# Norm attention layers: q and k turned by VectorE blocks and a DRAM trip, the score mask added on VectorE

## Chip, cores and metric

The kernel is one launch on one core of a Trainium2 chip. The metric is device time in microseconds, median over runs. TensorE is called PE below, VectorE DVE, ScalarE ACT, GpSimd POOL, and SyncE, which here issues most DMAs, SP.

## What is computed

Eight sublayers on `x` (8 batch elements b, 128 tokens, 512 columns): four times cross attention and a feed-forward part, each `x = x + tanh(g) * f(layernorm(x))`. The attention of layers 0, 1 and 3 has 32 query heads in 8 groups that share k and v, heads of 128. Layer 0 rotates q and k by position, layers 1 and 3 normalise them (layer 2 has small heads, and its code is another):

```python
q = rmsnorm((hidden_states @ q_proj_w.T).reshape(B, Q, NUM_HEADS, HEAD_DIM).transpose(0, 2, 1, 3), q_norm_w)
k = rmsnorm(jnp.repeat(k, n_rep, axis=1), k_norm_w)       # k, v from cross_attention_states
scores = jnp.einsum('bhqd,bhkd->bhqk', q, k) * scale + attention_mask
attn = jax.nn.softmax(scores.astype(jnp.float32), axis=-1).astype(q.dtype)
out = jnp.einsum('bhqk,bhkd->bhqd', attn, v)
return out.transpose(0, 2, 1, 3).reshape(B, Q, NUM_HEADS * HEAD_DIM) @ o_proj_w.T
```

The feed-forward parts are a LoRA mixture (0), a quantised matmul (1), and mixtures of experts with dispatch (2, 3).

## The kernel before

**Split operands.** Every fp32 operand of a matmul is kept as a high and a low part in fp32r: ACT copies the high part, DVE or POOL subtracts it from the source for the low part, and a product is three matmuls (high-high, high-low, low-high).

**Units.** In layers 0, 1 and 3 the work is cut into 64 units, unit u being group u // 8 and batch element u % 8: project q (4 heads), k and v into a PSUM bank pair (L806 by `keys_values` and `project`), normalise or rotate q and k into `qk` (L1592), transpose the five 128x128 pieces on PE (`turn_q`, four L852 into `B_qT` and one L855), split q and k into high and low (ACT L1162, DVE L1474 and L1615), scores (L863, L864), mask, maximum, exponentials (L1333), division by the sum (POOL L2222), turn P, P times v (L883), split of the result o, projection to the output (L806 into `B_out`) and addition to `X` (L1650).

**The mask.** ACT copies the low half of the scores, scaled, from PSUM to `S` (`low_scores`); POOL adds the mask (L2183); DVE adds the high half (`mask`, L1622) and takes the maximum (L1625).

**Turning P.** All but 8 units turn P without PE: DVE transposes blocks of 32x32 (`blocks_p`, L1640), SP stores them to DRAM (`store_p`, L2367) and loads them back in another order (`load_p`, L2372), ACT and POOL split the result (`split_p`, L2228).

**The order.** The class `Schedule` writes one order for all engines. Unit u has its home step i = first + u; `at(i, order, name, ...)` puts an operation into step i at a place between 0 and 100. One list comes out, sorted by step and place, and each engine takes from it the operations that it has a part in and runs them in that order, waiting on semaphores. So in a steady step i PE runs attn_out of unit u-6, times_v of u-5, scores of u-2, turn_q of u-1, and the projections of u. Operation `next` splits a landed half of a weight (256 KB; 10 halves each 8 units) and asks SP for the next; in steady steps one at place 15 gives the low part to DVE, one at 90 to POOL.

**Between stages** (the first and last 8 units of a layer), layer norms and feed-forward parts are put among the units.

## Time and profile before

| | us |
|---|---|
| median of 3 runs | 2618.07 (2617.1 to 2621.32) |
| span of the profiled execution | 2614.6 |
| PE busy | 2382.5 (91%) |
| DVE busy | 1786.3 (68%) |
| POOL busy | 1512.2 (58%) |
| ACT busy | 1278.9 (49%) |

Busy times are of the one profiled execution. Engines run side by side, so the times don't add up to the span, and a share over the whole span mixes stages with different limits. An engine that is busy all of a stretch is its bound there.

### The profile page before, as it was taken

The page shows a single profiled execution, that of the slowest core. Times are in us where ns is not written, and L with a number is a line of the kernel's source. Part 1 is how long each engine was busy: PE and PEld are TensorE (multiplying, and loading weights), DVE is VectorE, ACT ScalarE, POOL GpSimd, SP SyncE. Part 2 cuts the span into 40 slices and gives each one's busy share as a digit, 9 for nine tenths or more (in the row PEclk, how much of TensorE's full clock was granted, in tenths as well). Part 3 has the DMA queues.
Part 4 walks back from the last instruction along what each step waited for, and adds up shares of the span by engine and source line. Part 5 has one row for each costly group of instructions (what it writes and reads, how often), then busy time and mean ns, then how long its engine had stood idle before and what let it go on. Part 6 is the DMA issues. An engine that isn't in the chain of part 4 may idle for free.

```text
span 2614.6 us, 41410 instructions
## 1 busy us (share of the span) xinstructions
PE 2382.5 (91%) x13005; PEld 2016.6 (77%) x13005; DVE 1786.3 (68%) x3406; ACT 1278.9 (49%) x3698; POOL 1512.2 (58%) x1567
## 2 busy tenths in 40 slices
PE   5899999998889999999887887899689999999977
PEld 4788888886778888888766776776578888888753
DVE  4677777777877777777666676563477777777752
ACT  2555555554246666666534455233245666665421
POOL 5666666665246666666535667423456666666543
PEclk9999999999999999999999999899889999999979
DMA  3234444443224233223310000259513233322344
GB/s 110 80 118 155 141 160 159 151 162 109 71 84 142 97 98 102 93 93 98 109 49 17 1 1 27 81 193 365 175 61 108 91 98 101 101 94 77 116 169 151
DMA packets 191532, 288.12 MB, mean 110 GB/s; under 512 B 15985, under 2 KB 110833, under 8 KB 188378
## 3 DMA queue, kind: packets, MB, share of 16 engines
q1 hardware_dynamic: 175584, 236.34, 27.1%
q0 software_dynamic: 10224, 42.03, 4.6%
q10 hardware_dynamic: 5514, 7.11, 0.9%
q8 instruction: 112, 1.84, 0.3%
q14 instruction: 98, 0.80, 0.1%
HBM read 218.80 MB, written 100.37 MB: 122 GB/s over the span
## 4 chain that ended last, share of the span: by engine, by line
PE 73%; DVE 8%; DMA 6%; POOL 5%; issue 4%; ACT 3%; SPq 0%; POOLq 0%; ACTq 0%; DVEq 0%
PE B_qkv L806 32%; PE B_out L806 19%; PE B_more L883 4%; PE B_s L863 4%; PE B_qT L852 3%; DMA slots_y<-S 3%; PE B_more L806 2%; PE B_s L864 1%; PE B_more L957 1%; DMA out_x<-rows_last 1%; PE B_s L806 1%; DVE xn L1523 1%; DVE X L1650 1%; PE B_qT L806 1%; PE B_more L855 1%
## 5 line engine op out<-in xcount | busy, mean ns | idle before, releaser
L1333 ACT ACTIVATE W<-S,nmx 128x128 f32<-128x128 f32 x768 | 298.1, 395 | 49.9 <-DVE nmx L1625 48.8
L2183 POOL TENSOR_TENSOR S<-S,mask 128x512 f32<-128x512 f32 x184 | 256.6, 1394 | 46.9 <-ACT S L1162 46.9
L1226 ACT ACTIVATE sq<-B_qkv 128x640 f32<-128x640 f32 x127 | 89.7, 706 | 380.1 <-PE B_qkv L806 380.1
L2228 POOL TENSOR_TENSOR pT_l<-W,pT_h 128x512 fp32r<-128x512 f32 x184 | 241.8, 1314 | 32.9 <-ACT pT_h L1162 30.7
L2157 POOL TENSOR_SCALAR rn<-ss 128x5 f32<-128x5 f32 x128 | 25.3, 198 | 371.3 <-DVE ss L1563 371.3
L806 PE MATMUL B_qkv<-ring_h,xnT_h 128*128 128x512 f32 x540 | 216.2, 400 | 11.3 <-DVE spare_l L1474 4.8
L2222 POOL TENSOR_TENSOR W<-W,rden 128x512 f32<-128x512 f32 x192 | 202.1, 1052 | 32.7 <-DVE rden L1630 32.6
L806 PE MATMUL B_qkv<-ring_l,xnT_h 128*128 128x512 f32 x540 | 214.5, 397 | 0.0
L806 PE MATMUL B_out<-ring_h,oT_h 128*128 128x512 f32 x516 | 206.1, 399 | 8.7 <-DVE kT L1615 4.4
L806 PE MATMUL B_qkv<-ring_h,xnT_l 128*128 128x512 f32 x540 | 212.8, 394 | 0.0
L863 PE MATMUL B_s<-kT,qT_h 128*128 128x256 f32 x768 | 191.1, 326 | 17.8 <-DVE xnT_l L1474 15.1
L806 PE MATMUL B_out<-ring_l,oT_h 128*128 128x512 f32 x516 | 205.7, 399 | 0.0
L806 PE MATMUL B_out<-ring_h,oT_l 128*128 128x512 f32 x516 | 202.6, 393 | 0.0
L1563 DVE TENSOR_REDUCE ss<-sq 128x5 f32<-128x640 f32 x128 | 105.1, 821 | 140.8 <-ACT sq L1226 140.7
L1650 DVE SCALAR_TENSOR_TENSOR X<-B_out,gates,X 128x512 f32<-128x512 f32 x200 | 149.0, 745 | 42.3 <-PE B_out L806 42.3
L2149 POOL TENSOR_TENSOR ring_l<-raw,ring_h 128x512 fp32r<-128x512 f32 x107 | 144.2, 1351 | 50.4 <-ACT ring_h L1162 50.3
L864 PE MATMUL B_s<-kT,qT_l 128*128 128x128 f32 x768 | 172.0, 224 | 0.0
L1640 DVE STREAM_TRANSPOSE S<-W 128x512 f32<-128x512 f32 x184 | 129.4, 703 | 62.1 <-POOL W L2222 62.1
L863 PEld LDWEIGHTS B_s<-kT,qT_h 128*128 128x128 f32 x768 | 146.1, 190 | 29.5 <-issue 21.8
L1162 ACT ACTIVATE oT_h<-B_more 128x512 fp32r<-128x512 f32 x200 | 119.6, 598 | 97.6 <-PE B_more L883 94.6
L806 PE MATMUL B_qkv<-ring_h,ctxT_h 128*128 128x256 f32 x540 | 165.0, 306 | 0.0
L2160 POOL TENSOR_TENSOR rn<-rn,pw 128x5 f32<-128x5 f32 x128 | 151.1, 1181 | 10.7
(514 smaller groups left out, 7730.5 us busy)
## 6 DMA issues: line engine op xcount, KB each, us to landing
raw<-in_pieces SPq DMA_DIRECT2D x270, 256.0 KB, 2.6
between_p<-S SPq DMA_DIRECT2D x184, 256.0 KB, 2.2
W<-between_p SPq DMA_DIRECT2D x184, 256.0 KB, 2.8
slots_x<-in_zero SPq DMA_DIRECT2D x32, 1030.0 KB, 6.0
raw<-in_experts SPq DMA_DIRECT2D x16, 768.0 KB, 6.5
w<-in_experts SPq DMA_DIRECT2D x8, 1024.0 KB, 14.0
slots_y<-S SPq DMA_DIRECT2D x31, 256.0 KB, 6.4
xn<-slots_x ACTq DMA_DIRECT2D x8, 257.5 KB, 5.8
```

What stands on the lines that cost most here:

```text
L806: t = pe.matmul(dst, a, b, start=first and n == 0, stop=last and n == len(steps) - 1)
L863: pe.matmul(B_s[:, cols(r, 2 * P)], qT[0][:, cols(r)], kT_both[:, :], start=True, stop=False)
L864: t = pe.matmul(B_s[:, cols(2 * r)], qT[1][:, cols(r)], kT[0], start=False, stop=True)
L1162: return act.activation(dst, src, ACT.Copy, scale=scale)
L1333: t = act.activation(W[:, k, cols(r)], S[:, k, cols(r)], ACT.Exp, bias=nmx[:, k, r:r + 1], accum_out=den[:, k, r:r + 1])
L1640: dve.transpose(blocks_first(S[:, k, :]), W[:, k, :].rearrange("p (r j q) -> p r j q", r=R, q=BLOCK)).then_inc(*blocks_made.now((layer, u)))
L1650: dve.scalar_tensor_tensor(out=X[:, b, 0:D], in0=bank[:, :], scalar=factor, in1=X[:, b, 0:D], op0=ALU.mult, op1=ALU.add).then_inc(*x_add.n ...
L2149: pool.tensor_tensor(lo, landing_place(item), f32(hi), ALU.subtract).then_inc(*piece_lo["pool"].now(i))
L2160: pool.tensor_tensor(rn[:, k, 0:R + 1], rn[:, k, 0:R + 1], pw[:, 0:R + 1], ALU.pow).then_inc(*rms.now((layer, u)))
L2183: pool.tensor_tensor(S3, S3, m.unsqueeze(1).to_broadcast([P, R, P]), ALU.add).then_inc(*masked.now((layer, u)))
L2222: pool.tensor_tensor(W3, W3, rden[:, k, :].unsqueeze(2).to_broadcast([P, R, P]), ALU.mult).then_inc(*probs.now((layer, u)))
L2228: pool.tensor_tensor(heads_first(pT[1][:, :]), by_block(W[:, k, :]), heads_first(f32(pT[0][:, :])), ALU.subtract).then_inc(*p_split.now((l ...
```

## The change

For units 8 to 59 of layers 1 and 3 (`TURNED_BY_DMA`) q and k are no longer turned by PE. DVE transposes 32x32 blocks of `qk` into `xn` (`blocks_q`), SP stores them to DRAM and loads them back (`store_q`, `load_q`, 320 KB each, the load in runs of 640 bytes) into a new tile `q_in`. ACT scales k by the norm weights in place and copies the high parts, DVE makes k's low part, POOL q's (`split_q`). Their projections alternate between two bank pairs, `B_qkv` and the banks that `B_qT` and P's turning had. The order of these units is new: scores come behind the projection of two units later (place 70.5), mask and maximum at 4 of the next step, exponentials at 16, the block transpose and store of P at 42 of the same step. In these steps the weight split at place 15 goes to POOL.

For all units of layers 0, 1 and 3 ACT's copy of the low scores and POOL's addition of the mask are gone: DVE makes two passes from PSUM instead of one (scaled low half plus mask, then the high half), and the maximum stands in an operation of its own directly behind them.

Smaller parts: the 8 units whose P is turned by PE write their exponentials in turned order; the norm weights come in two orders of rows; the routers' weights are loaded later, and share their place with `q_in`; waits for the last q store and split stand ahead of what reuses `xn` and that place.

```diff
@@ -56,6 +56,8 @@
 AHEAD = tuple((0, u) for u in range(1, 5))
+TURNED_BY_DMA = {(layer, u) for layer in (1, 3) for u in range(NB, G * NB - 4)}
+LAST_BY_DMA = G * NB - 5
...
@@ -152,24 +154,42 @@
                 self.at(i + 1, 6 if layer == 1 and u < NB else 10, "normalise", layer, u)
-            self.at(i + 1, 50, "turn_q", layer, u)
-            self.at(i + 1, 50, "split_k", layer, u)
-            self.at(i + 2, 40, "scores", layer, u)
-            self.at(i + 2, 41, "low_scores", layer, u)
-            self.at(i + 2, 56, "mask", layer, u)
-            self.at(i + 2, 71, "exp", layer, u)
-            self.at(i + 3, 9, "probs", layer, u)
-            if (layer, u) in TURNED_BY_PE:
-                self.at(i + lag - 2, 46 if u == 0 and (layer, 1) in AHEAD else 30, "turn_p", layer, u)
+            if (layer, u) in TURNED_BY_DMA:
+                self.at(i + 1, 10.2, "blocks_q", layer, u)
+                self.at(i + 1, 12, "store_q", layer, u)
+                self.at(i + 1, 41, "load_q", layer, u)
+                self.turns_by_dma.add(i + 2)
+                self.at(i + 2, 13, "split_k", layer, u)
+                self.at(i + 2, 13.5, "split_q", layer, u)
+                self.at(i + 2, 70.5, "scores", layer, u)
+                self.at(i + 3, 4, "mask", layer, u)
+                self.at(i + 3, 4, "max", layer, u)
+                self.at(i + 3, 16, "exp", layer, u)
+                self.at(i + 3, 40, "probs", layer, u)
+                self.at(i + 3, 42, "blocks_p", layer, u)
+                self.at(i + 3, 42, "store_p", layer, u)
+                self.at(i + 3, 73, "load_p", layer, u)
+                self.at(i + 4, 45, "split_p", layer, u)
             else:
-                self.at(i + 3, 21, "blocks_p", layer, u)
-                self.at(i + 3, 21, "store_p", layer, u)
-                self.at(i + 3, 62, "load_p", layer, u)
-                self.at(i + lag - 2, 60, "split_p", layer, u)
+                self.at(i + 1, 72 if (layer, u - 1) in TURNED_BY_DMA else 50, "turn_q", layer, u)
+                self.at(i + 1, 72 if (layer, u - 1) in TURNED_BY_DMA else 50, "split_k", layer, u)
+                self.at(i + 2, 40, "scores", layer, u)
+                self.at(i + 2, 56, "mask", layer, u)
+                self.at(i + 2, 56, "max", layer, u)
+                self.at(i + 2, 71, "exp", layer, u)
+                self.at(i + 3, 9, "probs", layer, u)
+                if (layer, u) in TURNED_BY_PE:
+                    self.at(i + lag - 2, 46 if u == 0 and (layer, 1) in AHEAD else 30, "turn_p", layer, u)
+                else:
+                    self.at(i + 3, 21, "blocks_p", layer, u)
+                    self.at(i + 3, 21, "store_p", layer, u)
+                    self.at(i + 3, 62, "load_p", layer, u)
+                    self.at(i + lag - 2, 60, "split_p", layer, u)
             self.at(i + lag - 1, 20, "times_v", layer, u)
             self.at(i + lag, 0, "attn_out", layer, u, needs=five[3:5],
                     frees=[(n, "attn_out", (layer, u), i + lag) for n in five[3:5]] if last else ())
-            self.at(i + lag, 10.5 if KINDS[layer] == "norm" else 0, "add_out", layer, u)
+            self.at(i + lag, 10.5 if KINDS[layer] == "norm" else 0,
+                    "add_out", layer, u)
...
@@ -413,13 +433,23 @@
             for order in ((71, 90) if i < 7 else (15, 90) if i in self.steady else (5, 24, 46, 90)):
-                self.at(i, order, "next", i + order / 100, "dve" if order in (15, 46) else "pool")
+                if i in self.turns_by_dma and order == 15:
+                    self.at(i, order, "split_piece", i + order / 100)
+                    self.at(i, 42.5, "fetch_piece", i + order / 100)
+                else:
+                    self.at(i, order, "next", i + order / 100, "dve" if order == 46 else "pool")
         for i in range(end + 1):
             for _, _, name, args, needs, frees in sorted(self.events[i], key=lambda x: x[:2]):
                 if name == "next":
                     now, engine = args
...
@@ -593,18 +625,21 @@
         between_p = [nc.dram_tensor(f"between_p{k}", (P * HG,), F32).ap() for k in range(2)]
+        between_q = [nc.dram_tensor(f"between_q{k}", (P * (HG + P),), F32).ap() for k in range(2)]
         scales = [tables[:, :, :].rearrange("p a n -> p (a n)")[:, h * HALF:(h + 1) * HALF] for h in range(2)]
         B_qkv = pb("B_qkv", 1024)
-        B_qT = pb("B_qT", 512)[:, :]
         B_s = pb("B_s", 1024)
         B_sc, B_kT = B_s[:, 0:512], B_s[:, 512:1024]
-        B_more = pb("B_more", 1024)
-        B_pt, B_oT = B_more[:, 0:512], B_more[:, 512:1024]
+        B_three = pb("B_three", 1536)
+        B_qT, B_pt, B_oT = (B_three[:, k * 512:(k + 1) * 512] for k in range(3))
+        B_more, B_other = B_three[:, 512:1536], B_three[:, 0:1024]
         def unit_bank(layer, u):
-            return (B_more, ("pt", "oT")) if (layer, u) in ASIDE else (B_qkv, ("qkv",))
+            if (layer, u) in ASIDE:
+                return B_more, ("pt", "oT")
+            return (B_other, ("qT", "pt")) if u % 2 and (layer, u) in TURNED_BY_DMA else (B_qkv, ("qkv",))
...
@@ -1240,15 +1291,28 @@
                 kind = KINDS[layer]
-                act.wait_ge(*qk_turned.of((layer, u)))
+                by_dma = (layer, u) in TURNED_BY_DMA
+                act.wait_ge(*(q_loaded[unit(layer, u)[3]] if by_dma else qk_turned).of((layer, u)))
                 for sem, value in qT_reader:
                     act.wait_ge(sem, value)
                 if layer == 3 and u == 0:
                     act.wait_ge(*kbd_made2.of(NB - 1))
-                scale = wqk[:, layer // 2:layer // 2 + 1] if kind == "norm" else 1.0
+                scale = key_weights(layer, u) if kind == "norm" else 1.0
                 if kind == "norm" and u == 0:
                     act.wait_ge(*const.of("wqk"))
-                copy(key_rows(layer, u, kT[0]), key_columns(layer, u), scale).then_inc(*kT_hi.now((layer, u)))
+                if by_dma:
+                    if kind == "norm":
+                        copy(keys_in, keys_in, scale).then_inc(*k_scaled.now((layer, u)))
+                        act.wait_ge(*k_scaled.of((layer, u)))
+                    copy(keys_by_part(kT[0]), keys_in).then_inc(*kT_hi.now((layer, u)))
+                else:
+                    copy(block_keys(kT[0]), turned_keys(key_bank(layer, u)[0]), scale).then_inc(*kT_hi.now((layer, u)))
+            def split_q(layer, u):
+                act.wait_ge(*q_loaded[unit(layer, u)[3]].of((layer, u)))
+                for sem, value in qT_reader:
+                    act.wait_ge(sem, value)
+                copy(heads_first(qT[0][:, :]), queries_in).then_inc(*qT_hi.now((layer, u)))
...
@@ -1311,26 +1377,16 @@
-            def low_scores(layer, u):
-                k = unit(layer, u)[3]
-                act.wait_ge(*scored.of((layer, u)))
-                if layer == 0 and u == 0:
-                    act.wait_ge(*const.of("mask0"))
-                if layer == 3 and u < 2:
-                    for t in range(TILES2 - 2, TILES2):
-                        act.wait_ge(*y_stored[t % 2].of((2, t)))
-                elif k in S_reader:
-                    act.wait_ge(*S_reader[k])
-                copy(per_head(S[:, k, :]), score_parts[:, :, 1, :], SCALE).then_inc(*low_scored.now((layer, u)))
             def exp(layer, u):
                 kind, g, b, k, vs = unit(layer, u)
                 act.wait_ge(*maxed.of((layer, u)))
                 for token in W_reader.get(k, ()):
                     act.wait_ge(*token)
...
@@ -1604,23 +1665,54 @@
+            def blocks_q(layer, u):
+                k = unit(layer, u)[3]
+                dve.wait_ge(*{"rope": roped, "norm": normed}[KINDS[layer]].of((layer, u)))
+                if u == NB:
+                    dve.wait_ge(*ln_turned.of((f"attn{layer}", NB - 1)))
+                else:
+                    dve.wait_ge(*q_stored[1 - k].of((layer, u - 1)))
+                dve.transpose(blocks_first(q_turns), qk[:, :].rearrange("p (h j q) -> p h j q", j=BLOCKS, q=BLOCK)
+                              ).then_inc(*q_blocks.now((layer, u)))
             def split_k(layer, u):
+                kind = KINDS[layer]
+                if (layer, u) in TURNED_BY_DMA:
+                    turned, (hi, lo) = keys_in, (keys_by_part(m) for m in kT)
+                else:
+                    turned, (hi, lo) = turned_keys(key_bank(layer, u)[0]), (block_keys(m) for m in kT)
+                dve.wait_ge(*kT_hi.of((layer, u)))
+                if kind == "rope" or (layer, u) in TURNED_BY_DMA:
+                    sub(lo, turned, f32(hi)).then_inc(*kT_lo.now((layer, u)))
+                else:
+                    dve.scalar_tensor_tensor(out=lo, in0=turned, scalar=key_weights(layer, u), in1=f32(hi),
+                                             op0=ALU.mult, op1=ALU.subtract).then_inc(*kT_lo.now((layer, u)))
+            def mask(layer, u):
                 kind, g, b, k, vs = unit(layer, u)
-                bank = key_columns(layer, u)
-                hi, lo = (key_rows(layer, u, m) for m in kT)
-                dve.wait_ge(*kT_hi.of((layer, u)))
-                if kind == "rope":
-                    sub(lo, bank, f32(hi)).then_inc(*kT_lo.now((layer, u)))
-                else:
-                    dve.scalar_tensor_tensor(out=lo, in0=bank, scalar=wqk[:, layer // 2:layer // 2 + 1], in1=f32(hi),
-                                             op0=ALU.mult, op1=ALU.subtract).then_inc(*kT_lo.now((layer, u)))
-            def mask(layer, u):
+                S3 = per_head(S[:, k, :])
+                m = mask0[:, b, :] if kind == "rope" else mask13[:, :]
+                dve.wait_ge(*scored.of((layer, u)))
+                if layer == 0 and u == 0:
+                    dve.wait_ge(*const.of("mask0"))
+                if layer == 1 and u == 0:
+                    dve.wait_ge(*small["mask13"].of(0))
+                if layer == 3 and u < 2:
+                    for t in range(TILES2 - 2, TILES2):
+                        dve.wait_ge(*y_stored[t % 2].of((2, t)))
+                elif k in S_reader:
+                    dve.wait_ge(*S_reader[k])
+                S_reader[k] = (exped if (layer, u) in TURNED_BY_PE else p_stored[k]).of((layer, u))
+                dve.scalar_tensor_tensor(out=S3, in0=score_parts[:, :, 1, :], scalar=SCALE, in1=m.unsqueeze(1).to_broadcast([P, R, P]),
+                                         op0=ALU.mult, op1=ALU.add).then_inc(*low_masked.now((layer, u)))
+                dve.wait_ge(*low_masked.of((layer, u)))
+                dve.scalar_tensor_tensor(out=S3, in0=score_parts[:, :, 0, :], scalar=SCALE, in1=S3, op0=ALU.mult, op1=ALU.add
+                                         ).then_inc(*sc_read.now((layer, u)))
+            def largest(layer, u):
                 k = unit(layer, u)[3]
                 S3 = per_head(S[:, k, :])
-                dve.wait_ge(*masked.of((layer, u)))
-                dve.scalar_tensor_tensor(out=S3, in0=score_parts[:, :, 0, :], scalar=SCALE, in1=S3, op0=ALU.mult, op1=ALU.add
-                                         ).then_inc(*sc_read.now((layer, u)))
...
@@ -2168,19 +2261,10 @@
-            def low_scores(layer, u):
-                    pool.tensor_tensor(S3, S3, m.unsqueeze(1).to_broadcast([P, R, P]), ALU.add).then_inc(*masked.now((layer, u)))
+            def split_q(layer, u):
+                pool.wait_ge(*qT_hi.of((layer, u)))
+                pool.tensor_tensor(heads_first(qT[1][:, :]), queries_in, heads_first(f32(qT[0][:, :])), ALU.subtract
+                                   ).then_inc(*q_low.now((layer, u)))
...
@@ -2372,6 +2456,27 @@
+            def store_q(layer, u):
+                k = unit(layer, u)[3]
+                sync.wait_ge(*q_blocks.of((layer, u)))
+                if q_loaded[k].made:
+                    sync.wait_ge(q_loaded[k].sem, q_loaded[k].by * q_loaded[k].made)
+                sync.dma_start(between_q[k].rearrange("(p n) -> p n", p=P), q_turns).then_inc(*q_stored[k].now((layer, u)))
+            def load_q(layer, u):
+                k = unit(layer, u)[3]
+                sync.wait_ge(*q_stored[k].of((layer, u)))
+                if u > NB:
+                    sync.wait_ge(*q_low.of((layer, u - 1)))
+                    sync.wait_ge(*kT_lo.of((layer, u - 1)))
+                elif layer == 1:
+                    sync.wait_ge(*ffn0_done.of(NB - 1))
+                elif layer == 3:
+                    sync.wait_ge(*v_group2.of((NB - 1, G - 1)))
+                    sync.wait_ge(*logits.of(("ffn2", NB - 1)))
+                sync.dma_start(q_in[:, :, :], between_q[k].rearrange("(i p n) -> p i n", i=BLOCKS, p=P)
+                               ).then_inc(*q_loaded[k].now((layer, u)))
...
```

## Rows read from the trace of the kernel before

**Rows 1.** The page's first line.

```profile
span 2614.6 us, 41410 instructions
```

**Rows 2.** Busy us (x instructions) by stretch: PE, PEld, DVE, ACT, POOL; clock; DMA share; GB/s.

```profile
300.00:400.00 100.00, 100.00 (x576) 87.73 (x575) 71.89 (x140) 54.98 (x170) 67.29 (x63) 1.00 0.43 144
900.00:1000.00 100.00, 100.00 (x576) 87.69 (x575) 72.67 (x127) 60.52 (x177) 64.08 (x62) 1.00 0.28 88
2150.00:2250.00 100.00, 100.00 (x576) 87.69 (x575) 73.97 (x128) 61.55 (x179) 65.65 (x62) 1.00 0.29 95
```

**Rows 3.** The same view, between layers 0 and 1.

```profile
590.00:770.00 180.00, 149.12 (x801) 125.94 (x800) 141.44 (x334) 63.85 (x188) 71.46 (x86) 0.94 0.26 88
```

**Rows 4.** Timeline of PE (start us, us, engine, line, operation) around one unit's transposes.

```profile
1014.44 0.61 PE L852 MATMUL B_qT<-ident,qk 128*128 128x128 f32 x4
...
1015.12 0.28 PE L806 MATMUL B_qkv<-ring_lent_l,ctxT_h 128*128 128x256 f32 x1
1015.24 0.28 PE L806 MATMUL B_qkv<-ring_lent_h,ctxT_l 128*128 128x256 f32 x1
```

**Rows 5.** Timeline of ACT, the exponentials of two units in a row.

```profile
1002.03 0.40 ACT L1333 ACTIVATE W<-S,nmx 128x128 f32<-128x128 f32 x1
...
1011.09 0.40 ACT L1333 ACTIVATE W<-S,nmx 128x128 f32<-128x128 f32 x1
...
1012.62 0.62 ACT L1162 ACTIVATE ring_h<-raw 128x512 fp32r<-128x512 f32 x1
```

**Rows 6.** Timeline of DVE over one unit; in brackets the idle time before and its releaser.

```profile
1009.16 0.67 DVE L1622 SCALAR_TENSOR_TENSOR S<-B_s,S 128x512 f32<-128x512 f32 x1
1009.87 0.69 DVE L1625 TENSOR_REDUCE nmx<-S 128x4 f32<-128x512 f32 x1
1011.07 0.82 DVE L1563 TENSOR_REDUCE ss<-sq 128x5 f32<-128x640 f32 x1 [0.51 <-ACT sq L1226]
1011.80 0.28 DVE L1474 TENSOR_TENSOR v_l<-B_qkv,v_h 128x128 fp32r<-128x128 f32 x1
1012.76 0.18 DVE L1630 RECIPROCAL rden<-den 128x4 f32<-128x4 f32 x1 [0.68 <-ACT W L1333]
1013.47 0.82 DVE L1592 TENSOR_TENSOR qk<-B_qkv,rn 128x640 f32<-128x640 f32 x1 [0.53 <-POOL rn L2160]
1014.21 0.74 DVE L1650 SCALAR_TENSOR_TENSOR X<-B_out,gates,X 128x512 f32<-128x512 f32 x1
1014.87 0.68 DVE L1474 TENSOR_TENSOR ring_l<-raw,ring_h 128x512 fp32r<-128x512 f32 x1
1015.47 0.68 DVE L1474 TENSOR_TENSOR oT_l<-B_more,oT_h 128x512 fp32r<-128x512 f32 x1
1016.07 0.70 DVE L1640 STREAM_TRANSPOSE S<-W 128x512 f32<-128x512 f32 x1
...
1017.27 0.33 DVE L1615 SCALAR_TENSOR_TENSOR kT<-B_more,wqk,kT 128x128 fp32r<-128x128 f32 x1
```

**Rows 7.** Timeline of DVE and POOL, a weight split beside a POOL instruction.

```profile
1005.60 1.04 POOL L2222 TENSOR_TENSOR W<-W,rden 128x512 f32<-128x512 f32 x1
...
1005.82 1.37 DVE L1474 TENSOR_TENSOR ring_l<-raw,ring_h 128x512 fp32r<-128x512 f32 x1
```

**Rows 8.** Groups of 800 to 1200 us: busy us, mean ns, idle before.

```profile
L2183 POOL TENSOR_TENSOR S<-S,mask 128x512 f32<-128x512 f32 x44 | 67.6, 1537 | 13.9 <-ACT S L1162 13.9
...
L2228 POOL TENSOR_TENSOR pT_l<-W,pT_h 128x512 fp32r<-128x512 f32 x45 | 58.3, 1295 | 1.1 <-ACT pT_h L1162 0.7
...
L1162 ACT ACTIVATE pT_h<-W 128x512 fp32r<-128x512 f32 x44 | 27.8, 633 | 0.9 <-DMA W<-between_p 0.9
```

**Rows 9.** SP's timeline of one trip of P, and time to landing of the loads.

```profile
1008.44 0.33 SPq L2367 DMA_DIRECT2D between_p<-S  x1
1010.49 0.38 SPq L2372 DMA_DIRECT2D W<-between_p  x1
...
DMA to landing us min/median/max: 2.5/2.7/5.8
```

93 lines of the change are left out of this document (57 added, 36 removed).

## Prediction

> **What bounds the kernel now.** I read the page's first section, then busy time by stretch, then the timelines of one unit (one batch element of one group of heads), engine by engine, then the waits and DMA landings. The span is 2614.6 us [rows 1]; the median of the runs is 2618.07, so 3.5 us more. By stretch [rows 2] TensorE (PE) is busy 100.00 of 100.00 us in the middle of layers 1 and 3, at a granted clock of 1.00 (the 2.4 GHz level), while VectorE (DVE) has 73 to 74, ScalarE (ACT) about 61 and GpSimd (POOL) about 65. So there only less work on PE saves time, until another engine or a loop of waits needs longer than PE. Between stages [rows 3] it is the other way round: in 590 to 770 PE loses 31 us and DVE is busy 141 of 180.
> One unit takes 9.06 us: ACT's exponentials start at 1002.03 and, one unit on, at 1011.09 [rows 5].
>
> **PE, the gain.** A unit now has five transposes, four L852 and one L855. The first starts at 1014.44; the second matmul of the projection behind them starts at 1015.12 [rows 4]; L855 and the first matmul lie between. Matmuls of 256 columns follow each other by 0.12 (1015.12 to 1015.24), so the five take 1015.12 - 0.12 - 1014.44 = 0.56 us. They go in units 8 to 59 of layers 1 and 3: 2 x 52 = 104 units, 104 x 0.56 = **58 us**. All of it lies where PE is the bound. A unit of PE alone would then take 9.06 - 0.56 = **8.50 us**. Moving scores behind the next projection adds no PE work; the alternating second bank lets the projection start without the normalisation before it.
>
> **DVE's loop, the first thing that may come late.** DVE works in order, and the block transpose of P (blocks_p) now stands in the same step as the exponentials it follows. From one reduction of squares to the next, in the new order, start to start from [rows 6]: reduction 0.73, v low 0.21, two mask passes 0.71 each (0.67 and a gap of 0.04 since each waits for the one before), maximum 0.62, normalisation 0.86 (0.82 and the gap; otherwise a start comes 0.07 before the end of the one ahead), new blocks_q 0.81 (640 columns where the shown transpose has 512 and 0.70: 0.88, less 0.07 overlap), add to X 0.66, k low 0.25, o low 0.60, reciprocal 0.18, then POOL's 1.04 [rows 7] with 0.12 for its two semaphores (an estimate from the 0.04 gap on DVE, taken larger since it crosses engines), blocks_p 0.62. Sum **8.12 us**. The second mask pass is bounded by its like, the pass of L1622 at 0.67, and by the 0.74 of L1650, also PSUM with SBUF. The exponentials (1011.09 to the next ACT instruction at 1012.62: 1.53 [rows 5]) start when the maximum is out, and o's copy follows them, about 2.1 in all; DVE has 0.86 + 0.81 + 0.66 + 0.25 = 2.58 to do meanwhile, so "o behind the exponentials" is covered with 0.4 to spare. Were this cover gone, each late 0.1 us would count.
> Also gone from DVE: q's low part and its share of weight splits (now all POOL's in these units).
> An unknown: k's low part now reads two SBUF operands. DVE's weight split with two SBUF operands took 0.68 alone and 1.37 when a POOL instruction was under way [rows 6, 7]. POOL gets the weight splits and q's low part (by its like, L2228, 1.30) and loses the mask addition of 1.54 [rows 8]: -1.54 + 1.30 + about 0.6 splits of 1.30 = +0.54 a unit, on about 65 / 100 x 9.06 = 5.9, so 6.4 busy of 8.5. Bounds of the wait: 0 and a whole POOL instruction of 1.30. I take 0.4 on average, since a POOL split stands at that place in about 6 of 10 units: 8.12 + 0.4 = 8.52, about PE's 8.50. **Taken: 8.52 a unit, 104 x (9.06 - 8.52) = 56 us saved.**
> The Trainium skill (SBUF — State Buffer, "SBUF: two separate sides") says that a DVE instruction with two SBUF inputs and a GpSimd instruction that reads SBUF exclude each other, the later one waiting for the whole of the other. The trace agrees: 0.68 against 1.37. By the rule k's low part, 0.33 with a PSUM source, could take up to 1.6.
>
> **The trip's loop, the second.** ACT's split_k and split_q now stand before the exponentials, so ACT waits for the loaded q with the exponentials behind it; on them hang DVE's reciprocal, blocks_p, the next reduction and two steps later blocks_q. That closes a loop over two units: reduction to the end of blocks_q 4.72; store 2.05 for P (issue 1008.44, the waiting load at 1010.49 [rows 9]), taken 2.2 for a quarter more bytes; load 2.7 [rows 9], taken 2.9; ACT's k scaling, k copy and q copy 1.3 (an estimate: P's copy of the same 512 columns takes 0.63, k's with 128 about half [rows 8]); exponentials 1.53, o's copy 0.67, then o low, reciprocal, POOL, blocks_p 2.56. Sum 15.9 in two units, **8.0 a unit**: hidden by 0.5 a unit. Bounds for the load: 2.5 and 5.8, the shortest and longest of P's. SP is queued too: store_q, load_q, store_p, the weight load, load_p; behind store_q's wait stand the weight loads, but each of its two trips blocks it about 2.2 us, and it then has 4 us for its other issues of 0.33 to 0.38. Scores (PE) want q's low part about 7.7 into the loop; POOL has it at about 5.
>
> **The mask, all 192 units.** ACT's copy and POOL's addition go, DVE gets 0.67. Inside the full stretches it is in the 8.12; in layer 0 DVE goes from 71.89 / 100 x 9.06 = 6.5 to 7.2 a unit, hidden. In the ramps between stages it isn't surely hidden: about 38 units lie there, 38 x 0.67 = 25 us if all of it counts; below nothing, -5, if the shorter way to the maximum matters more (DVE waited there only a few us for POOL's mask addition). I take 7, about ten units at the 79% busy DVE of 590 to 770. The exponentials' turned writes in 8 units, the wider constants, the late load of the routers: nothing, in shade of PE.
> **Entering and leaving** the new order, four times: bounds 0 and 3 us each (one late DMA trip); I take 3 in all.
>
> **Sum.** -56 + 7 + 3 = -46: the profiled span 2614.6 becomes 2569, the median 2618.07 becomes **2572**.
>
> **Rivals.**
> *Port.* k's low part meets POOL in every unit and waits half an instruction, 0.65: 8.77 a unit, 104 x 0.29 = 30 saved, -30 + 10: **2598**. For it: POOL is busy three quarters of the time. Against: outside the splits POOL is idle just then. The rule cited above makes this one; it needs only the rows.
> *The trip comes late (slower).* If store and load need 7.3 us together instead of 5.1, the two-unit loop is 18.1 and the gain gone; from there it costs. With loads at P's longest, 5.8, it is 18.9: 9.43 a unit, 104 x 0.37 = +38, with the ramps +10: **2666**. For it: a weight load may be on the wire with each, and SP's order lets a late weight split hold back store_q. Against: P's own trips show a median of 2.7 with the same weight loads about, and the DMA share is 0.29 [rows 2].
> *The ramps eat it.* The full 25 us there and 4 x 3 for entering: -56 + 37: **2599**.
> *Nothing in the way.* 58 saved, ramps -2: **2558**.
>
> **Chances.** Forecast (2560 to 2590) 0.52, port 0.14, ramps 0.10, nothing in the way 0.06, late trip 0.12, and 0.06 that several small losses add up to no change. A measurement here can tell 0.2%, 5 us, from no change. Late trips split 0.10 slower and 0.02 same; the small losses 0.05 same and 0.01 slower; 0.01 same and 0.03 slower come out of the port and ramp cases at their upper ends. So faster 0.78, same 0.08, slower 0.14. The range reaches from below the free case to just over no change: 2555 to 2622; the likeliest one's own is 2560 to 2590.
>
> **What would show it.** PE matmuls in a full 100 us stretch: 52 a unit become 47; at 8.5 us a unit 553 instead of 576 matmuls, PE still near 100. If PE is under 98 there, a loop binds: then look at what PE waits for. Waits of ACT's k copy for the DMA into q_in mean the late trip; k's low part over 0.5 us on DVE means the port; reductions directly behind blocks_p with no idle time mean DVE's loop. Between stages, DVE's share and PE's lost time tell the ramps. I would be wrong most of all if the unit stays over 8.8.

## The result, and the profile after

The changed kernel takes 2585.5 us (median of 4 runs, 2585.0 to 2594.8) beside 2619.4 us of the kernel before on the same chip: ratio 0.9885, 95% interval 0.9867 to 0.9903, which is 25 to 35 us of 2619 (the medians lie 34 apart). The forecast was 2572, 46 us faster. The profiled execution's span went from 2614.6 [rows 1] to 2584.0, 30.6 us; the account below is made against that.

From the page of the changed kernel: first line, busy time by engine, the chain that ended last by engine, and the DMA issues (count, KB each, us to landing):

```profile
span 2584.0 us, 40807 instructions
PE 2344.7 (91%) x12485; PEld 1968.5 (76%) x12485; DVE 1860.3 (72%) x3505; ACT 1231.8 (48%) x3610; POOL 1480.0 (57%) x1572
...
PE 21%; POOL 13%; DMA 12%; DVE 10%; issue 9%; ACT 4%; SPq 0%; POOLq 0%; DVEq 0%; ACTq 0%
...
between_p<-S SPq DMA_DIRECT2D x184, 256.0 KB, 2.5
W<-between_p SPq DMA_DIRECT2D x184, 256.0 KB, 2.8
between_q<-xn SPq DMA_DIRECT2D x104, 320.0 KB, 2.6
q_in<-between_q SPq DMA_DIRECT2D x104, 320.0 KB, 3.0
```

The chain is no longer one engine's: PE's share was 73% before. Busy time by stretch, the columns of rows 2 and the stretches of rows 2 and 3:

```profile
300.00:400.00 100.00, 100.00 (x576) 87.68 (x575) 75.87 (x144) 48.71 (x157) 59.40 (x58) 1.00 0.45 143
900.00:1000.00 100.00, 100.00 (x549) 86.26 (x548) 84.98 (x141) 64.74 (x189) 74.11 (x73) 1.00 0.54 172
2150.00:2250.00 100.00, 98.76 (x537) 84.53 (x536) 82.21 (x137) 61.79 (x180) 75.27 (x74) 1.00 0.56 174
...
590.00:770.00 180.00, 152.76 (x833) 129.98 (x833) 142.28 (x351) 61.38 (x188) 61.08 (x79) 0.96 0.27 90
```

PE is still at 99 to 100, with 549 and 537 matmuls in 100 us where a unit now has 47 (52 and 576 before [rows 2]): 8.56 and 8.75 us a unit. DVE has risen from 73 and 74 to 85 and 82, the DMA share from 0.28 and 0.29 to 0.54 and 0.56. In the stretch between layers 0 and 1 PE is busy 3.6 us more than in rows 3, so nothing was lost there. One correction to the working: the weight split at place 15 is GpSimd's in all steady steps, layer 0's too, and with it DVE has 75.9 there and not 79.

The length of a unit is read best from the start of DVE's normalisation of q and k. For units 12 and 54 of layer 1, changed kernel:

```profile
842.54 0.81 DVE L1653 TENSOR_TENSOR qk<-B_qkv,rn 128x640 f32<-128x640 f32 x1
...
1203.98 0.82 DVE L1653 TENSOR_TENSOR qk<-B_qkv,rn 128x640 f32<-128x640 f32 x1
```

(1203.98 - 842.54) / 42 = 8.606 us; layer 3 gives 8.620; before it was 9.053 in both. The same reading over the whole kernel gives the account of the 30.6 us. "Steady" is units 12 to 54; negative is time won:

The forecast column takes 9.053 less 8.52 for each unit.

| stretch | layer 1 | layer 3 | forecast, both |
|---|---|---|---|
| up to unit 0 | +2.6 | (in "behind" of layer 1) | |
| units 0 to 8 | -2.3 | -0.2 | +7 mask, in all ramps |
| units 8 to 12 | +0.8 | -0.7 | -4.3 |
| steady, 12 to 54 | -18.8 | -18.2 | -44.8 |
| units 54 to 59 | +5.5 | -2.2 | -5.3 |
| units 59 to 63 | +2.5 | +3.1 | |
| behind | +0.9 | -3.7 | |
| entering, leaving | in the rows above | in the rows above | +3 |

So the steady part won 37.0 of 44.8, the 18 units next to it (8 to 12 and 54 to 59) lost 3.4 where 9.6 should have been won, and all the other rows together cost 2.9 where 10 were feared.

The table is of one execution. In a second profiled one of the same order (e5 below) the steady part won 32.3, the 18 units beside it lost 1.8, and all other rows cost 1.8. So the steady part's share is safe to about 5 us, and a single row of the ramps to about 2: units 0 to 8 of layer 1, -2.3 here, are 0.0 there.

**TensorE's own pace.** In an undisturbed unit scores follow scores by 1018.23 - 1009.68 = 8.55 us (timeline of PE, changed kernel):

```profile
1009.68 0.28 PE L911 MATMUL B_s<-kT,qT_h 128*128 128x256 f32 x1
...
1018.23 0.28 PE L911 MATMUL B_s<-kT,qT_h 128*128 128x256 f32 x1
```

Of the 82 such distances in the steady parts 47 are 8.55. Five transposes are therefore worth 9.05 - 8.55 = 0.50, not 0.56, and what lies between 8.55 and the mean of 8.61 are single late units: at DVE the 42 of layer 1 lie between 8.0 and 9.4, and the longest of layer 3 is 10.1.

**DVE's loop**, one unit of the changed kernel (the sequence that the forecast summed):

```profile
1003.46 0.78 DVE L1624 TENSOR_REDUCE ss<-sq 128x5 f32<-128x640 f32 x1
1004.15 0.28 DVE L1532 TENSOR_TENSOR v_l<-B_three,v_h 128x128 fp32r<-128x128 f32 x1
1004.35 0.68 DVE L1707 SCALAR_TENSOR_TENSOR S<-B_s,mask 128x512 f32<-128x512 f32 x1
1005.06 0.69 DVE L1710 SCALAR_TENSOR_TENSOR S<-B_s,S 128x512 f32<-128x512 f32 x1
1005.79 0.69 DVE L1717 TENSOR_REDUCE nmx<-S 128x4 f32<-128x512 f32 x1
1006.39 0.81 DVE L1653 TENSOR_TENSOR qk<-B_three,rn 128x640 f32<-128x640 f32 x1
1007.24 0.84 DVE L1676 STREAM_TRANSPOSE xn<-qk 128x640 f32<-128x640 f32 x1
1008.01 0.71 DVE L1742 SCALAR_TENSOR_TENSOR X<-B_out,gates,X 128x512 f32<-128x512 f32 x1
1008.64 0.59 DVE L1532 TENSOR_TENSOR kT<-q_in,kT 128x128 fp32r<-128x128 f32 x1
1009.16 0.67 DVE L1532 TENSOR_TENSOR oT_l<-B_three,oT_h 128x512 fp32r<-128x512 f32 x1
1009.76 0.15 DVE L1722 RECIPROCAL rden<-den 128x4 f32<-128x4 f32 x1
1011.06 0.71 DVE L1732 STREAM_TRANSPOSE S<-W 128x512 f32<-128x512 f32 x1 [1.15 <-POOL W L2306]
1011.70 0.78 DVE L1624 TENSOR_REDUCE ss<-sq 128x5 f32<-128x640 f32 x1
```

8.24 us from reduction to reduction, with one wait, the 1.15 for GpSimd. The shortest unit of the trace is 8.02. The group of k's low part (busy us, mean ns), 0.77 us in the mean of 104:

```profile
L1532 DVE TENSOR_TENSOR kT<-q_in,kT 128x128 fp32r<-128x128 f32 x104 | 80.0, 769 | 0.0
```

**The trips.** SP's issues over one unit (timeline of SP):

```profile
1008.11 0.32 SPq L2464 DMA_DIRECT2D between_q<-xn  x1
1010.30 0.37 SPq L2477 DMA_DIRECT2D q_in<-between_q  x1
1011.80 0.32 SPq L2451 DMA_DIRECT2D between_p<-S  x1
...
1014.37 0.37 SPq L2456 DMA_DIRECT2D W<-between_p  x1
```

and ACT, which takes what they brought (its timeline over two units):

```profile
1004.90 0.54 ACT L1210 ACTIVATE q_in<-q_in,wqk 128x128 f32<-128x128 f32 x1 [2.77 <-DMA q_in<-between_q]
...
1006.85 0.39 ACT L1389 ACTIVATE W<-S,nmx 128x128 f32<-128x128 f32 x1
...
1013.75 0.53 ACT L1210 ACTIVATE q_in<-q_in,wqk 128x128 f32<-128x128 f32 x1 [2.48 <-DMA q_in<-between_q]
1015.77 0.63 ACT L1210 ACTIVATE ring_h<-raw 128x512 fp32r<-128x512 f32 x1 [0.51 <-DMA raw<-in_pieces]
```

q leaves at 1008.11 and ACT starts on it at 1013.75, 5.6 us later. Over the 75 units of 850 to 1180 and 2010 to 2330 the same two readings give 5.8 in the mean (2.7 to the load's issue, 3.1 to its use), 5.0 at the least and 7.3 at the most. SP, which works in order, can issue nothing while it waits for the store.

In the second of these two units q's copy ends at 1015.26, after the maximum, then ACT waits for a weight, and the exponentials start 1.6 us after the maximum's end. What follows, from the timelines of ACT, POOL and DVE:

```profile
1014.03 0.69 DVE L1717 TENSOR_REDUCE nmx<-S 128x4 f32<-128x512 f32 x1
1016.30 0.39 ACT L1389 ACTIVATE W<-S,nmx 128x128 f32<-128x128 f32 x1
...
1016.59 1.30 POOL L2242 TENSOR_TENSOR ring_l<-raw,ring_h 128x512 fp32r<-128x512 f32 x1
1016.88 1.17 DVE L1532 TENSOR_TENSOR kT<-q_in,kT 128x128 fp32r<-128x128 f32 x1
1018.45 0.69 DVE L1532 TENSOR_TENSOR oT_l<-B_three,oT_h 128x512 fp32r<-128x512 f32 x1 [0.40 <-ACT oT_h L1210]
```

GpSimd's split of the late weight ends at 1017.89, and k's low part, begun before that, at 1018.05; o's copy comes 0.40 late. This unit takes 9.32 us at DVE. Over the 84 steady units q's copy ends after the maximum in 69, and the exponentials start 0.75 us after it in the mean. Where they start over 0.5 late (57 units) the unit is 8.87 and k's low part 0.96, in the other 27 units 8.08 and 0.41 (e5: 8.94 and 8.05). So ACT's lateness, from q and from weights, goes with the long units; that is read from the traces, and no run takes all of it away.

### The profile page after: what moved, and what is told of

It is laid out like the page before. It is cut to its first block, busy times and chain, and to the rows that moved or that the text cites. A ratio compares the mean times of both kernels' runs of the same rounds, so it can differ in the third digit from the quotient of the medians.

```text
span 2584.0 us, 40807 instructions
## 1 busy us (share of the span) xinstructions
PE 2344.7 (91%) x12485; PEld 1968.5 (76%) x12485; DVE 1860.3 (72%) x3505; ACT 1231.8 (48%) x3610; POOL 1480.0 (57%) x1572
## 4 chain that ended last, share of the span: by engine, by line
PE 21%; POOL 13%; DMA 12%; DVE 10%; issue 9%; ACT 4%; SPq 0%; POOLq 0%; DVEq 0%; ACTq 0%
PE B_qkv L854 6%; PE B_out L854 4%; DMA q_in<-between_q 3%; DMA between_q<-xn 3%; PE B_three L854 3%; DMA slots_y<-S 3%; POOL qT_l L2266 2%; POOL ring_l L2242 2%; POOL W L2306 2%; DVE ss L1624 2%; POOL rn L2253 2%; DVE qk L1653 1%; DMA out_x<-rows_last 1%; PE B_three L1005 1%; POOL ring_lent_l L2242 1%
## 5 line engine op out<-in xcount | busy, mean ns | idle before, releaser
L2242 POOL TENSOR_TENSOR ring_l<-raw,ring_h 128x512 fp32r<-128x512 f32 x166 | 214.9, 1297 | 62.6 <-ACT ring_h L1210 62.4
L911 PEld LDWEIGHTS B_s<-kT,qT_h 128*128 128x128 f32 x768 | 148.0, 193 | 55.3 <-issue 47.8
L854 PE MATMUL B_qkv<-ring_h,xnT_h 128*128 128x512 f32 x408 | 164.5, 403 | 11.4 <-DVE spare_l L1532 4.8
L1210 ACT ACTIVATE q_in<-q_in,wqk 128x128 f32<-128x128 f32 x104 | 55.4, 532 | 243.3 <-DMA q_in<-between_q 243.3
L1532 DVE TENSOR_TENSOR oT_l<-B_three,oT_h 128x512 fp32r<-128x512 f32 x200 | 136.3, 682 | 47.8 <-ACT oT_h L1210 47.1
L2260 POOL TENSOR_TENSOR qk<-sq,qk 128x320 f32<-128x320 f32 x64 | 56.1, 877 | 193.3 <-DVE qk L1641 193.3
L2266 POOL TENSOR_TENSOR qT_l<-q_in,qT_h 128x512 fp32r<-128x512 f32 x104 | 134.9, 1297 | 55.4 <-ACT qT_h L1210 54.5
L854 PE MATMUL B_qkv<-ring_l,xnT_h 128*128 128x512 f32 x408 | 162.5, 398 | 0.0
L854 PE MATMUL B_qkv<-ring_h,xnT_l 128*128 128x512 f32 x408 | 161.0, 395 | 0.0
L912 PEld LDWEIGHTS B_s<-kT,qT_l 128*128 128x128 f32 x768 | 150.2, 196 | 5.4
L1210 ACT ACTIVATE ring_h<-raw 128x512 fp32r<-128x512 f32 x190 | 116.2, 625 | 66.7 <-DMA raw<-in_pieces 40.6
```

The source lines that it names most:

```text
L854: t = pe.matmul(dst, a, b, start=first and n == 0, stop=last and n == len(steps) - 1)
L911: pe.matmul(B_s[:, cols(r, 2 * P)], qT[0][:, cols(r)], kT_both[:, :], start=True, stop=False)
L912: t = pe.matmul(B_s[:, cols(2 * r)], qT[1][:, cols(r)], kT[0], start=False, stop=True)
L1210: return act.activation(dst, src, ACT.Copy, scale=scale)
L1532: return dve.tensor_tensor(dst, a, b, ALU.subtract)
L2242: pool.tensor_tensor(lo, landing_place(item), f32(hi), ALU.subtract).then_inc(*piece_lo["pool"].now(i))
```

## The experiments

The theory after the first look: TensorE's 8.55 is the floor, and three loops stand close above or below it: DVE's order, q's trip by way of ACT, and SP's queue. Rivals: the price of the mask in the ramps, the shared port, the ends of the layers. The column "unit" is units 12 to 54, the mean of layers 1 and 3; ratios are to the kernel before on the same chip.

| run | what is different | ratio, 95% interval | unit |
|---|---|---|---|
| the change | | 0.9885 [0.9867, 0.9903] | 8.61 |
| e1 | mask part alone | 1.0006 [0.9993, 1.0019] | 9.05 |
| e2 | before, less 4 of 5 transposes | 0.9864 [0.9847, 0.9882] | 8.68 |
| e3 | k's low part on GpSimd | 0.9864 [0.9843, 0.9885] | 8.67 |
| e4 | q loaded twice | 1.1018 [1.0994, 1.1041] | 11.57 |
| e5 | the change once more | 0.9879 [0.9862, 0.9895] | 8.67 |
| e6 | k's low part twice | 0.9970 [0.9955, 0.9985] | 8.87 |
| e7 | layer 1 by DMA to unit 52 only | 0.9894 [0.9876, 0.9912] | 8.63 (layer 3) |
| e8 | e7 once more | 0.9888 [0.9867, 0.9908] | 8.64 (layer 3) |
| e9 | addition to X ahead of blocks_p | 0.9921 [0.9906, 0.9937] | 8.74 |
| e10 | exponentials ahead of k's and q's copies | 1.0352 [1.0329, 1.0374] | 9.93 |
| e11 | a quarter of k's low part | 0.9873 [0.9852, 0.9893] | 8.72 |
| e12 | weight's copy behind the exponentials | 0.9871 [0.9847, 0.9894] | 8.61 |

The change and e5 are the same program in order: their units differ by 0.06 and their ratios by 0.0006. Nothing smaller than that is read from single runs below.

**The mask part alone.** The changed kernel with an empty set of units turned by DMA:

```
-TURNED_BY_DMA = {(layer, u) for layer in (1, 3) for u in range(NB, G * NB - 4)}
+TURNED_BY_DMA = set()
```

> The changed kernel with no unit turned by DMA: q and k go over PE's transposes everywhere, as before. What is left of the change is the mask on VectorE in all 192 units, and the weight split of the steady steps given to GpSimd. Theory (the mask is hidden where PE is full and costs a little in the ramps): against the kernel before +7 us, 0 to +12. Rival (the ramps pay every pass, 38 x 0.67): +25 us. Rival (the shorter way to the maximum wins): -5 us. In the full stretches 9.05 us a unit in all of them.

Measured: 2619.3 beside 2617.0, no difference that can be told. The unit stays at 9.053. By the trace units 54 to 63 of layer 1 got 4.7 us longer, where DVE also works on the next layer's quantised weights; e7 and e8, which have the old order there too, show 4.3 and 5.2. So the mask costs DVE time in that ramp. Units 0 to 8 of layer 1 got 2.8 us shorter (112.4 for 115.2), where the maximum no longer waits for ACT's copy and GpSimd's addition; but the kernels below, which all have this mask, take 112.6 to 116.9 there, so a gain in that ramp is not shown.

**Transposes alone.** The kernel before, which leaves out four of q's five transposes (so its q is wrong) in the units that the change turns by DMA:

```
-                for h in range(R):
+                for h in range(R if layer == 0 or not NB <= u < G * NB - 4 else 0):
                     pe.transpose(B_qT[:, cols(h)], qk[:, cols(h)], ident[:, :])
```

> The kernel before, but in units 8 to 59 of layers 1 and 3 the four transposes of q are left out (q's splits read what the bank held; the fifth, k's, stays). Theory (PE is the only bound there, a transpose is 0.11 us of it): 104 x 4 x 0.11 = 47 us less, 8.6 us a unit, 2572. Rival (an engine or a wait next to PE stops it earlier): under 30 us less, and PE shows idle time in the full stretches.

Measured: the unit is 8.68, each transpose 0.375 / 4 = 0.094. This kernel has no new loop, keeps PE at 100.00 of 100.00, and wins the same 34 us as the whole change: by its trace 33.3, of which 31.5 in the steady parts, where the change won 37.0 there and 30.6 in all. In units 54 to 59 it wins 1.9 in layer 3 and only 0.1 in layer 1: two of those units take 14.2 and 13.6 us in the kernel before, and PE is busy 16.1 and 17.3 of 20 us in the two stretches of 1235 to 1275, so the transposes are not what bounds them. Five would give 0.47; the changed kernel's 8.55 says 0.50. The forecast's reading of one unit [rows 4] gave 0.112 each; why those stood further apart isn't settled.

**k's low part on GpSimd** instead of DVE:

```
                 if (layer, u) in TURNED_BY_DMA:
-                    turned, (hi, lo) = keys_in, (keys_by_part(m) for m in kT)
...
+                    return
...
+                if (layer, u) in TURNED_BY_DMA:
+                    hi, lo = (keys_by_part(m) for m in kT)
+                    pool.wait_ge(*kT_hi.of((layer, u)))
+                    pool.tensor_tensor(lo, keys_in, f32(hi), ALU.subtract).then_inc(*k_low.now((layer, u)))
```

> The changed kernel with k's low part of the DMA units on GpSimd instead of VectorE. Port theory (VectorE's loop of 8.63 us a unit binds, and 0.65 of it is k's low part, waiting for GpSimd's port): VectorE's loop falls to 8.0, PE's 8.50 binds, 104 x 0.13 = 13 us less than the changed kernel, about 2572. Trip theory (ScalarE waits for q's load and the exponentials behind it set the pace): no change from 2585.5, or a few us more since GpSimd gets 0.5 us a unit.

Measured: no gain over the change. DVE has 0.77 less to do and waits instead; waits of 850 to 1200 (us in total, times, longest):

```profile
DVE oT_l L1532 <- ACT oT_h L1210: 35.9, 33, 2.8
```

In the changed kernel the same wait is 5.4 in 400 us. ACT comes to o's copy behind q's copies and the exponentials, so ACT's order, tied to the landing of q, is right behind DVE's.

**q loaded twice**, the second load waiting for the first:

```
+                               ).then_inc(*q_once.now((layer, u)))
+                sync.wait_ge(*q_once.of((layer, u)))
+                sync.dma_start(q_in[:, :, :], between_q[k].rearrange("(i p n) -> p i n", i=BLOCKS, p=P)
+                               ).then_inc(*q_loaded[k].now((layer, u)))
```

> The changed kernel, and SP loads q and k twice in a row, the second load waiting for the first: the trip is 3.0 us longer. If the trip's loop over two units is hidden behind VectorE's by 2 x 0.6 us, (3.0 - 1.2) / 2 = 0.9 us a unit, +94 us, 2680. If the trip binds already: 3.0 / 2 = 1.5 us a unit, +156 us, 2741. If it is well hidden (the loop closes otherwise than I think): under +20 us.

Measured: +2.96 a unit, nearly the whole second load (3.09 from the first load's issue to the second's) and twice what a loop over two units could charge. What SP waited for between 850 and 1200, 30 units:

```profile
SPq L2457 <- DMA between_p<-S: 91.4, 31, 4.4
SPq L2481 <- DMA q_in<-between_q: 80.4, 30, 3.7
SPq L2478 <- DMA between_q<-xn: 63.7, 30, 3.9
```

235 us in 30 units, 7.8 a unit, and beside them only 1.0 for an engine (for q's low part, while q's store is under way); the rest of the 11.57 are the issues. SP's queue is full, a third loop, over one unit. In the changed kernel SP waits for landings 128.5 us in 41 units, 3.1 each, and 3.2 each for engines; 1.0 of these is for k's low part and runs beside q's store, so some 2.2 us of a unit are free there and SP isn't the bound. The second load put 2.7 on top, and each store that SP waits out became dearer (P's from 1.9 to 3.0, q's from 1.2 to 2.1 a unit), since it lands later: P's 3.75 us after its issue in the mean where it was 2.54, q's 3.53 for 2.65. P's store now goes out 0.5 behind the second load, where 1.5 lay between them before; that this is why it lands later is not shown. All three cases of the expectation missed this run's size.

**The addition to X later, first attempt.** It asks a set that holds no step that far ahead when it is asked, so no engine's order changed:

```
-            self.at(i + lag, 10.5 if KINDS[layer] == "norm" else 0,
+            self.at(i + lag, 40.5 if i + lag in self.turns_by_dma else 10.5 if KINDS[layer] == "norm" else 0,
```

> The changed kernel, but in the steps of the new order the addition to X stands directly ahead of P's block transpose, where VectorE waits for GpSimd's normalisation of P (49.6 us in 43 waits of 400 us), and no longer ahead of the maximum's successors. VectorE's loop loses the 0.63 us of the addition. If VectorE's loop sets the unit's 8.61: the unit falls to TensorE's own 8.55, 84 steady units x 0.06 = 5 us less, and the stalls ahead of the scores go. If SP's queue or the q trip sets it (its loop doesn't hold the addition): no change, 2585. A third way: the reader of B_out's bank then frees it some 2 us later, and TensorE waits for it in the next output projection: slower, up to 84 x 0.3 = 25 us.

It is the changed kernel once more, and says how far two of its runs lie apart.

**k's low part twice** on DVE, the second behind the first:

```
+                if (layer, u) in TURNED_BY_DMA:
+                    sub(lo, turned, f32(hi)).then_inc(*k_once.now((layer, u)))
+                    dve.wait_ge(*k_once.of((layer, u)))
```

> The changed kernel with the low part of k computed twice on VectorE in the 104 units turned by DMA, the second after the first. One is 0.33 us when GpSimd is quiet and 0.73 in the mean. If VectorE's loop is what stands next to TensorE's 8.55 (its least unit 8.02 to 8.24): the loop gets 8.6 to 9.0, and the unit grows by 0.1 to 0.4: 10 to 42 us slower, 2595 to 2627. If SP's queue and its landings are next (some 2 us away from 8.6 by the waits of the changed kernel) and VectorE has room: under 5 us.

Measured: 2612.3 beside 2620.7. The shortest unit is 8.43, 0.41 more than 8.02, and the mean unit 8.87, 0.20 to 0.25 more. DVE's loop is near: of the 0.43 that the second instruction takes in the mean about 0.2 are free, the rest counts, and PE is at 98.8 and 97.2 in the two full stretches.

**Layer 1 by DMA only to unit 52**, so that DVE's quantised weights meet the old order:

```
-TURNED_BY_DMA = {(layer, u) for layer in (1, 3) for u in range(NB, G * NB - 4)}
-LAST_BY_DMA = G * NB - 5
+LAST_BY_DMA = {1: G * NB - 11 - 1, 3: G * NB - 5}
+TURNED_BY_DMA = {(layer, u) for layer in (1, 3) for u in range(NB, LAST_BY_DMA[layer] + 1)}
```

> The changed kernel, with layer 1 turned by DMA only to unit 52 instead of 59, so that the units beside which VectorE takes the low parts of the next layer's quantised weights keep the old order. Seven units then pay PE's transposes again, 7 x 0.45 = +3 us where TensorE binds. Theory: in units 54 to 63 of layer 1 the changed kernel lost 8.0 us against before (60.8 + 49.0 against 55.3 + 46.5), because VectorE's loop is fuller there; these go: net -5 us, 2580. Rival (the loss is from the change of order itself, which then comes earlier): +3, 2588.

> Both edits together: layer 1 turned by DMA to unit 52 and the addition to X directly ahead of P's block transpose. If each gives what the theory of a full VectorE says: -5 and -5, 2575. If SP's queue binds in the steady part: the one of layer 1's end alone, 2580. If neither: 2588.

(The second has the ineffective edit of e5, so it is this kernel again.) Measured: 2591.8 and 2589.0 beside 2620.7, no gain. Units 54 to 59 fell from 60.8 (58.9 in e5) to 57.4 and 58.4, which is what the mask alone gives (e1: 57.8, before: 55.3), but units 12 to 54 rose by 7 us, of which only 1 is transposes: leaving the new order costs some us wherever it is done. The times fit the rival. The dear units of layer 1's end in the changed kernel are two of 16.0 and 16.2 us, which had been 14.2 and 13.6. In the first of them DVE stands at the zeros of a quantised weight, with two mask passes, the maximum and k's low part queued behind; PE's scores wait 12.4 us for k's low part in these two units. From the timeline of the changed kernel:

```profile
1225.93 0.69 DVE L1601 TENSOR_TENSOR raw<-raw 128x512 f32<-128x512 int32 x1 [4.74 <-DMA raw<-in_zeros]
```

**The addition to X directly ahead of P's block transpose**, where DVE waits 1.15 us for GpSimd:

```
+            self.at(i + lag, 40.5 if (layer, u + lag - 2) in TURNED_BY_DMA else 10.5 if KINDS[layer] == "norm" else 0,
```

> The changed kernel with the addition to X directly ahead of P's block transpose in the steps of the new order, which the edit of e5_add_late was meant to do: there it left every engine's order as it was, since the set that it asked holds no step that far ahead yet, and so that run is the changed kernel once more (and e8 is e7 once more). VectorE waits 1.15 us there for GpSimd, so the addition (0.63) becomes free and the loop of 8.24 falls to about 7.6; o's low part then stands 0.6 earlier and may wait for ScalarE's copy. If VectorE's loop, disturbed now and then, makes the 0.06 above TensorE's 8.55: 84 x 0.06 = 5 us less, 2582. If the stalls come from GpSimd's low part of q or from SP: 2587, no change. If TensorE then waits for B_out: slower, up to 25 us.

Measured: 2596.7 beside 2617.9, a ratio 0.004 above the change's and e5's, some 10 us slower. DVE's wait for GpSimd halved (22.2 us for 49.6 in 400 us), the shortest unit fell to 7.78, and the mean rose to 8.74. The time went into waits for ACT, and PE now waits for the bank that the later addition frees (waits of 800 to 1200):

```profile
DVE oT_l L1532 <- ACT oT_h L1210: 40.2, 41, 2.7
...
PE B_out L854 <- DVE X L1742: 3.7, 6, 1.1
```

**The exponentials ahead of ACT's copies of k and q:**

```
-                self.at(i + 3, 16, "exp", layer, u)
+                self.at(i + 3, 12.9, "exp", layer, u)
```

> The changed kernel with the exponentials ahead of ScalarE's copies of k and q in the steps of the new order; the other engines' orders stay. In the trace of the changed kernel the maximum is out at 1006.39 and the exponentials would end at 7.95; k's two copies then end at 8.9, q's at 9.4, o's at 9.9, where VectorE wants k's at 8.64 and o's at 9.16. If VectorE's loop is the near one: it waits 0.4 and 0.4 to 0.7, 8.24 becomes 9.0, 84 x (9.0 - 8.6) = 34 us slower, 2620, and more where q's low part comes too late for the scores. If the exponentials' wait for the loaded q (the trip's loop) is what binds: faster, 2580. If TensorE alone binds and all else has room: no change, 2587.

Measured: +1.3 a unit, three times the forecast. Waits of 800 to 1200:

```profile
ACT W L1389 <- DVE nmx L1717: 161.6, 38, 5.0
POOL qT_l L2266 <- ACT qT_h L1210: 118.2, 38, 3.9
...
PEld B_s L911 <- POOL qT_l L2266: 54.1, 37, 2.0
PE B_s L911 <- POOL qT_l L2266: 38.8, 34, 1.6
```

DVE's waits grew by about as much as expected (13.7 and 35.4 us in 38 units for k's and o's copy). The rest is a loop that the order closes: the maximum of one unit releases its exponentials, behind them come the next unit's copies of q, GpSimd's low part, that unit's scores on PE, its mask passes and its maximum. With the copies ahead of the exponentials, as the change has them, that loop is open. So the order "split_k, split_q, exp" that the forecast counted as a cost is what makes the change work.

**A quarter of k's low part.** DVE computes it for 32 of 128 columns (the scores are wrong for the others):

```
-                if kind == "rope" or (layer, u) in TURNED_BY_DMA:
+                if (layer, u) in TURNED_BY_DMA:
+                    sub(lo[:, 0:1], turned[:, 0:1], f32(hi)[:, 0:1]).then_inc(*kT_lo.now((layer, u)))
+                elif kind == "rope":
                     sub(lo, turned, f32(hi)).then_inc(*kT_lo.now((layer, u)))
```

> The changed kernel; VectorE's low part of k is computed for a quarter of the columns only in the 104 units turned by DMA (so the scores are wrong there; the work is left out to see what it costs). It takes 0.73 us in the mean, of which about 0.1 stays. If VectorE's loop makes what the unit has above TensorE's own 8.55: 84 x 0.06 = 5 us less, and 2 or 3 more at the ends of the layers: 2580. If it has room: 2587. It can't give more than TensorE's bound: below 2577 would say that five transposes are worth more than the 0.50 a unit that the spacing of the matmuls says.

Measured: 2586.7 beside 2617.9, no gain, the unit 8.72. But it gave DVE little room: the instruction takes 0.19 at the least and 0.61 in the mean, only 0.16 less than in the change, since the wait for GpSimd (0.42) stays as it was. So it is e3 and e9, with 0.77 and 0.63 less for DVE, that show nothing won, not this run. Its longest unit, 11.4 us, shows what stands next. ACT's timeline first, then busy time by stretch:

```profile
1099.18 0.62 ACT L1210 ACTIVATE qT_h<-q_in 128x512 fp32r<-128x512 f32 x1
1102.34 0.63 ACT L1210 ACTIVATE ring_lent_h<-raw 128x512 fp32r<-128x512 f32 x1 [2.53 <-DMA raw<-in_pieces]
1102.87 0.39 ACT L1389 ACTIVATE W<-S,nmx 128x128 f32<-128x128 f32 x1
```

```profile
1100.00:1105.00 5.00, 3.45 (x20) 2.86 (x18) 1.55 (x3) 2.66 (x11) 2.46 (x2) 1.00 0.55 173
1105.00:1110.00 5.00, 4.23 (x12) 3.33 (x13) 3.76 (x8) 3.26 (x7) 3.75 (x5) 0.66 0.53 156
```

The maximum was out at 1099.11 and q's copy at 1099.74, but ACT first waits for a weight whose load SP had issued only at 1099.78, behind P's trip. The exponentials start 3.1 us late, PE is busy 3.45 of 5, and the next 5 us have a granted clock of 0.66.

**That copy behind the exponentials:**

```
-                    self.at(i, order, "split_piece", i + order / 100)
+                    self.at(i, 16.5, "split_piece", i + order / 100)
```

> The changed kernel with ScalarE's share of the weight split (the copy ring_h from raw, 0.52 us in about 6 of 10 units) behind the exponentials instead of ahead of them in the steps of the new order. The other engines' orders stay. Theory from the traces so far: q's trip from store to use takes 5.8 us in the mean (5.0 to 7.3) where 5.1 was forecast, so the loop over two units is about 16.9, 8.45 a unit, within 0.1 of TensorE's 8.55, and every late landing, of q or of a weight on which that copy waits with the exponentials behind it (up to 2.5 us), stretches a unit to 9 or 10. Then this edit takes 0.31 + the waits for weights out of the loop: the steady unit goes from 8.61 - 8.72 to 8.57 - 8.60, 2 to 8 us less, about 2582. Rival (VectorE's loop makes the long units): no change, 2587. A third way: GpSimd's low part of the weight, now 0.7 later, runs into its normalisation of P: 0.1 to 0.3 a unit, 2595 to 2610.

Measured: 2586.7 beside 2616.8, a change against 2585.5 that can't be told from none. The steady unit is 8.570 in layer 1 and 8.652 in layer 3, the longest 9.7 in place of 10.1 (10.7 in e5), and 900 to 1100 us have 1101 matmuls for 1091. That is the direction of the theory in layer 1 and within the spread in layer 3: its size stays open. k's low part falls from 0.77 to 0.49 in the mean, and the unit doesn't follow: its wait for GpSimd isn't the bound either. So does how the last 0.06 to 0.1 a unit divides between late weights and late q.

## Why the prediction was right, and where it was off

**PE.** That five transposes were on the path: right, e2 wins 34 us by them alone. Their size was not: 0.50 (0.47 by e2) for 0.56. The floor is 8.55 where the sum had 8.50 for PE and took 8.52 for DVE's loop: 0.03 x 104 = 3 us. That the 8.52 lies so near the floor is partly luck, since it was DVE's number and PE is what binds.

**DVE's loop.** The order and nearly each step came as summed: 8.12 forecast without a wait, 8.02 in the shortest unit. The wait of k's low part was taken at 0.4: it is 0.769 - 0.361 (the shortest of the 104) = 0.41. The longest is 1.40, 1.04 above the shortest, less than GpSimd's whole 1.30. The Trainium skill (SBUF — State Buffer, "SBUF: two separate sides") has the later of the two wait for the rest of the other's instruction, and these numbers agree. So the loop was 8.02 + 0.41 = 8.43, where 8.52 was forecast; near PE's, but not the bound: e3 and e9 take 0.77 and 0.63 from it and win nothing, e12 takes 0.28 of the wait for GpSimd and wins nothing that can be told, e6 adds 0.4 and loses half of it. The port rival would have needed a wait of 0.65.

**The trip's loop** was forecast at 15.9 us over two units, hidden by 0.5 a unit. By the rows above: reduction to the end of blocks_q 4.6; store and load 5.8 (forecast 5.1); ACT's three copies 1.43 (1.3); ACT's copy of a weight, 0.5 in 6 of 10 units, 0.3, which was left out; exponentials and o's copy 2.1; o low 0.6; reciprocal to blocks_p 1.3; blocks_p 0.6. Sum 16.7, 8.4 a unit: hidden by 0.15 in the mean instead of 0.5, and not for trips of 7.3, which as in the rival's text is where the gain would be gone; but of 75 trips only two are over 7.1. This sum is argued from rows; what was shown is that ACT is next once DVE has room (e3, e9: DVE's waits for o's copy).

**SP** was said to have 4 us beside two blocks of 2.2. It waits 3.1 for both landings and 3.2 for engines, about as said, with some 2.2 free; e4 shows that one more landing uses this up and turns its queue into the loop, which no rival named.

**The mask in the ramps**, taken at 7 between -5 and +25: e1 gives 1.5 by the trace and a ratio of 1.0006 [0.9993, 1.0019] by the runs, -2 to +5 us. The +4.7 at the end of layer 1 is shown three times (e1, e7, e8); where it is won back is not shown. The rival "ramps eat it" falls.

**Entering and leaving**, taken at 3 in all, was too small, and so was the cost of the first and last units: units 8 to 12 lost 0.1 instead of winning 4.3, units 54 to 59 lost 3.3 instead of winning 5.3, of which 2.5 are the mask's (e1), and 59 to 63 lost 5.6, of which 2.4 are the mask's. The step that was mis-sized is "104 x", with its reason, "all of it lies where PE is the bound": only the 84 steady units earn the rate. In units 54 to 59 of layer 1, 55.3 us before and so 11.1 each, where DVE takes in the quantised weights, PE isn't the bound, and e2, with no new order, wins 0.1 there. The others pay for the change of order (e7) and for DVE's waits in order (the 4.74 above); in units 8 to 12 e2 wins 3.0 where the change loses 0.1.

Together, of the 15 us that the span is short of 46: 7.8 in the steady units (2.5 PE's floor, 5.3 late units; in e5 the late ones are 10), 13.0 in the 18 beside them, 1.6 because unit intervals are 102 and 9.053, less 7.1 that the mask and the ramps were cheaper. The last has the other sign, so part of the nearness of 2572 to 2585.5 is luck: without it the forecast would have been some 22 us off in the span.

Of the marks named ahead, the matmuls of a full stretch (549 for 553) and PE near 100 said PE's floor; the reductions directly behind blocks_p were there, though DVE's loop isn't the bound; k's low part is at 0.77, over the 0.5 that was to mean the port, and the port rival is wrong all the same. ACT's waits for q were there (112 us in 45 units), and by themselves say little: in the first of the two units shown q's wait ends at 1004.90, 1.5 us before the maximum is out, and costs nothing, in the second it ends at 1013.75, and q's copy comes 0.5 us after the maximum. The copy's end against the maximum's is the mark to use.

## What to carry to other kernels

Work taken off a saturated engine is worth what the distance of the units falls by without it. Here the starts of one unit said 0.56, and it was 0.50; leaving the work out (e2) measures it before the rest is built, and shows too in which units nothing is to be won. When several loops come within 0.2 us of each other, sum each of them, SP's queue too, and count only the units away from the ends; giving one loop room then wins nothing and may lose, as e9 did. In an in-order engine, put what waits for a DMA where nothing on the loop stands behind it, and what the next unit's loop needs ahead of what releases this one's: the second was worth 1.3 us a unit here (e10), the first no more than could be told (e12).

## What the runs showed of the hardware

- With q's trips the DMA share of 900 to 1000 us goes from 0.28 to 0.54, and P's own store, which was unchanged, lands in 2.5 us (the page's median) where it took 2.2; its load stays at 2.8. In e4, with two loads of 320 KB, P's store lands in 3.75 in the mean and held SP up to 4.4 us.
- An instruction of DVE that reads two SBUF operands took 0.36 to 1.40 us for 128 columns, beside GpSimd instructions of 1.30. A second one directly behind it was seldom caught: in e6 the first takes 0.71 in the mean and the second 0.43.
- 5 us in which PE was idle for 1.55 were followed by 5 us at a granted clock of 0.66 (e11). In the two full stretches e4, with PE busy 84 and 87%, has a granted clock of 0.95 and 0.92, and e10, with 89 and 93%, 0.98 and 0.97, where the change has 1.00. How much of the time of e4 and e10 is due to the clock, no run separates.
